# Paged attention behind three projections: the own keys' transpose in another place and another bank

## The chip, the cores and the metric

The kernel runs on one core of a Trainium2 chip, in one launch. The metric is the device time of that launch in microseconds. Before the change it is 2624.65 us, the median of three runs (2623.74 to 2630.95).

## The reference

`x` holds 64 sequences of 32 tokens of 512 numbers, in float32. Four layers are added to it, one after the other: a product with one of 8 weights for each sequence, two layers with low-rank adapters, and an attention layer. Only the last matters here:

```python
q = _rope(_rmsnorm(q, q_norm_w), pos)            # 32 query heads of 128
k = _rope(_rmsnorm(k, k_norm_w), pos)            # 8 key heads
kc = k_cache[block_table].reshape(bsz, L, HK, D) # 16 pages of 32 keys: L = 512
vc = v_cache[block_table].reshape(bsz, L, HK, D)
k_all = jnp.concatenate([kc, k], axis=1)         # 512 cached keys, then 32 own ones
v_all = jnp.concatenate([vc, v], axis=1)
scores = jnp.einsum('bqhd,bkhd->bhqk', q, k_all) * SCALE
scores = jnp.where(valid[:, None, None, :], scores, -1e+30)
probs = jax.nn.softmax(scores, axis=-1)
o = jnp.einsum('bhqk,bkhd->bqhd', probs, v_all)
return jnp.einsum('bse,de->bsd', o.reshape(bsz, seqlen, HQ * D), Wo)
```

## The kernel before, in words

The kernel has one program for each engine and sets all order by hand: each program is a list of instructions and of waits on semaphores, which other engines' instructions count up when they are done. I call such a count a mark.

The attention works in *units*: one sequence and one key head with its four query heads, so 128 rows of queries against 544 keys (512 cached, 32 own). There are 64 sequences x 8 heads = 512 units. The loop `pair` does two sequences, 16 units, in one turn (`in_pairs` writes the first and the last turn out and loops over the 30 between). I call one unit's share of each engine's program a *step*, and the 8 steps of one sequence a *half*, steps 0 to 7. In the code, `j` runs from 0 to 15, so step 7 is `j` = 7 or 15; behind `j` = 15 the loop turns. Units are taken in groups of four (`OG`): steps 0 to 3 and 4 to 7.

In step j TensorE (`tensor`, L1565 on) does:

- the scores of the unit two ahead (`scores`, L1348; three passes of a split product in each of two halves of the keys, L101 to L103). They go to bank pair j % 2 of `ps_s`; columns 384 to 511 of each bank are free of scores,
- the products of probabilities and values of the unit four behind (`outputs`, L1586; L1597 for cached keys, L1600 for own ones), into `ps_o`,
- the transposes of the probabilities of unit j against the cached keys (`transpose`, L1569; L1574), into `ps_pt`. In steps 3 and 7 the *own transpose* follows (L1580): the probabilities of the group's four units against their 32 own keys, which VectorE has gathered in `p_own`. It writes the spare columns of the odd bank pair (`spare`, L1254), and must not do so while VectorE reads that pair, hence the wait for `masked` (L1578). In step 7 the sums of the half's probabilities are transposed as well (`total`, L1582).

VectorE (`vector`) masks the scores of the unit two ahead and takes their maximum in one instruction (`mask_and_max`, L1319, named `att_prob<-both_ps_s,att_mask`), ahead of it gathers the own keys' probabilities of the unit one ahead (`gather`, L1508), splits keys and queries into a high and a low part (L1293), and copies finished outputs (L1530). At the start of steps 4 and 0 it copies the own transpose of the group before to `pto` (`copy_own`, L1515), and in step 0 it inverts the transposed sums into `inv` (`invert`, L1522). ScalarE takes the exponential (L1298), copies the transposed probabilities (L1476) and rounds the high parts (L1287).

GpSimd (`gpsimd`) issues, for each sequence in turn: the next queries and own keys (L1394, L1400), the next own values (L1412, four transfers), for which it waits until all products of the sequence before are done (`pv_done`, L1405), then four indirect gathers of the next values' pages (L1418), then the stores of the finished sequence (L1424, L1427). SyncE loads pages of keys. The last product of a sequence is done in step 3 of the next half.

The lines that matter for the waits are these:

```python
if j % OG == 3 and later(u, OG + 3):                     # scores, unit u = two ahead
    pe.wait_ge(pto_ready, UNITS // OG * i + j // OG)
if h == 3 and later(u, HK + 3):
    pe.wait_ge(inv_ready, 2 * i + p)
```

The first layer reads, on each engine, lists of places and adapters from memory into registers (`entries`, L191); on TensorE that is done once for four tiles.

## Time and profile before

| what | value |
| --- | --- |
| median of three runs | 2624.65 us (2623.74 to 2630.95) |
| span of the profiled execution | 2632.1 us |
| its mean granted TensorE clock | 0.979 of full speed |
| TensorE busy | 2449.5 us, 93% of the span |
| VectorE busy | 1799.6 us, 68% |
| ScalarE busy | 1587.4 us, 60% |
| GpSimd busy | 643.5 us, 24% |
| mean busy share of the 16 DMA engines, stretch 1400 to 1600 us | 0.82 |

The profile is of one execution, whose span, first to last instruction, is 2632.1 us; that is 7.5 us above the median of the timed runs and just above the slowest of them. A change of the sum that is made against the profiled execution is therefore carried over to the median as a difference. Times in the timelines are microseconds from the span's start. The attention fills the stretch from some 940 to 2235 us. The start of a TensorE row is taken from the hardware, its end is modelled, and matmuls overlap, so the length of a step is read from the start of one unit's scores to the start of the next one's.

### The profile page before, as it was taken

Reading aid. Unit: us, or ns where it says so; the run is one execution under the profiler, and the core shown is the slowest. Engines: PE = TensorE matmul, PEld = TensorE weight load, DVE = VectorE, ACT = ScalarE, POOL = GpSimd, SP = SyncE. Lnnn points to the kernel's source line nnn. Section 1 sums busy time; section 2 is a strip of 40 time slices with the busy share of each in tenths; the row PEclk is TensorE's granted clock in tenths of the full one; section 3 lists DMA queues with packets and bytes.
Section 4 is the critical chain, followed back from the end, with each engine's and each line's share of the span. In section 5 each row is a group of like instructions: output and inputs, shape, how many; then the busy total and the mean of one; then the engine's idle time right before and its main releaser. Section 6 shows DMA issues by size and latency. Waiting matters only on the chain. (4 is left out here: it accounts for less than half of the span.)

```text
span 2632.1 us, 55771 instructions
## 1 busy us (share of the span) xinstructions
PE 2449.5 (93%) x16326; PEld 2204.1 (84%) x16327; DVE 1799.6 (68%) x3690; ACT 1587.4 (60%) x3313; POOL 643.5 (24%) x932
## 2 busy tenths in 40 slices
PE   6799899999999889999999999999999999499999
PEld 5688688888888789999999998999999999388887
DVE  6445438999898967777777777777777776544443
ACT  3222237777787777777777777777777776311111
POOL 1222030000000134434443444344433442000000
PEclk9899899999999989999999999999999999799999
DMA  6422432333334388887888888887888883766664
GB/s 230 143 78 76 147 125 85 117 99 99 112 101 131 112 290 275 276 274 261 267 284 272 263 269 272 283 265 259 278 277 267 264 271 133 269 208 215 218 216 152
DMA packets 376143, 541.56 MB, mean 206 GB/s; under 512 B 49395, under 2 KB 263091, under 8 KB 372211
## 3 DMA queue, kind: packets, MB, share of 16 engines
q1 hardware_dynamic: 303922, 316.33, 37.9%
q0 software_dynamic: 70016, 221.30, 24.5%
q10 hardware_dynamic: 2112, 2.89, 0.4%
q8 instruction: 34, 0.56, 0.1%
q14 instruction: 59, 0.48, 0.1%
HBM read 442.06 MB, written 98.30 MB: 205 GB/s over the span
## 5 line engine op out<-in xcount | busy, mean ns | idle before, releaser
L1298 ACT ACTIVATE att_prob<-att_prob,att_shift 128x544 f32<-128x544 f32 x512 | 383.2, 748 | 262.2 <-DVE att_shift L1319 239.8
L1597 PE MATMUL both_ps_o<-att_pt,att_v 128*128 128x128 f32 x4096 | 540.0, 275 | 0.0
L1597 PEld LDWEIGHTS both_ps_o<-att_pt,att_v 128*128 128x128 f32 x4096 | 504.9, 191 | 0.0
L1319 DVE CUSTOM_DVE_ANT_0 att_prob<-both_ps_s,att_mask 128x544 f32<-128x544 f32 x512 | 365.5, 714 | 0.0
L101 PE MATMUL both_ps_s<-att_k_hi,att_q_hi 128*128 128x272 f32 x1024 | 340.5, 333 | 6.7 <-DVE att_k_lo L1293 5.2
L1293 DVE TENSOR_TENSOR att_k_lo<-att_k_raw,att_k_hi 128x1024 fp32r<-128x1024 f32 (+1 forms) x320 | 337.8, 1055 | 2.0 <-ACT att_k_hi L1287 1.9
L1476 ACT ACTIVATE att_pt<-both_ps_pt 128x512 f32<-128x512 f32 x512 | 296.8, 580 | 47.0 <-remote 43.6
L1574 PE MATMUL both_ps_pt<-both_ident,att_prob 128*128 128x128 f32 x2048 | 309.2, 274 | 7.6 <-ACT att_prob L1298 6.0
L1508 DVE COPY att_p_own<-att_prob 128x32 f32<-128x32 f32 x512 | 91.9, 180 | 324.6 <-PE both_ps_s L103 154.9
L1412 POOL DMA_DIRECT2D att_vo<-v_own x256 | 140.1, 547 | 651.8 <-PE both_ps_o L1600 589.1
L103 PE MATMUL both_ps_s<-att_k_hi,att_q_lo 128*128 128x272 f32 x1024 | 297.8, 291 | 0.0
L102 PE MATMUL both_ps_s<-att_k_lo,att_q_hi 128*128 128x272 f32 x1024 | 295.8, 289 | 0.0
L1287 ACT ACTIVATE att_k_hi<-att_k_raw 128x1024 fp32r<-128x1024 f32 (+1 forms) x320 | 292.9, 916 | 0.0
L1418 POOL DMA_INDIRECT att_v<-in_v_pages,att_rows_now x256 | 251.6, 983 | 85.9 <-issue 85.9
L1574 PEld LDWEIGHTS both_ps_pt<-both_ident,att_prob 128*128 128x128 f32 x2048 | 242.5, 142 | 8.3 <-ACT att_prob L1298 6.3
L101 PE MATMUL out_ps_y<-out_w_hi,out_o_hi 128*128 128x512 f32 x512 | 203.1, 397 | 37.3 <-DVE out_w_lo L1773 31.9
L1753 ACT ACTIVATE out_o_hi<-out_o 128x2048 fp32r<-128x2048 f32 x32 | 61.4, 1918 | 290.9 <-DVE out_o L1780 282.5
L101 PEld LDWEIGHTS both_ps_s<-att_k_hi,att_q_hi 128*128 128x128 f32 x1024 | 195.2, 191 | 16.9 <-issue 9.2
L102 PE MATMUL out_ps_y<-out_w_lo,out_o_hi 128*128 128x512 f32 x512 | 202.0, 395 | 0.0
L103 PE MATMUL out_ps_y<-out_w_hi,out_o_lo 128*128 128x512 f32 x512 | 201.8, 394 | 0.0
L1600 PE MATMUL both_ps_o<-att_pto,att_vo 128*128 128x128 f32 x1024 | 198.6, 276 | 2.4 <-DVE att_pto L1515 2.4
L102 PEld LDWEIGHTS both_ps_s<-att_k_lo,att_q_hi 128*128 128x128 f32 x1024 | 196.4, 192 | 0.0
(191 smaller groups left out, 5169.0 us busy)
## 6 DMA issues: line engine op xcount, KB each, us to landing
att_k_raw<-in_k_pages SPq DMA_DIRECT2D x1024, 128.0 KB, 3.9
q_t<-qkv_out_t SPq DMA_DIRECT2D x128, 256.0 KB
att_q_raw<-q_t POOLq DMA_DIRECT2D x64, 512.0 KB, 7.1
o_t<-att_o POOLq DMA_DIRECT2D x64, 512.0 KB, 6.9
out_o<-o_t SPq DMA_DIRECT2D x32, 1024.0 KB, 6.7
out_inv<-inv_t SPq DMA_DIRECT2D x32, 1024.0 KB, 6.7
qkv_w_stage<-in_w_qkv SPq DMA_DIRECT2D x12, 1024.0 KB, 5.2
l_w_stage<-in_w SPq DMA_DIRECT2D x8, 1024.0 KB, 6.8
```

Of the source, the lines that this page charges most:

```text
L101: pe.matmul(out, xh, wh, start=start, stop=False)
L102: pe.matmul(out, xh, wl, start=False, stop=False)
L103: return pe.matmul(out, xl, wh, start=False, stop=stop)
L1287: act.activation(hi, raw, ACT.Copy).then_inc(hi_done, 1)
L1293: dve.tensor_tensor(lo, raw, f32(hi), ALU.subtract).then_inc(lo_done, 1)
L1298: act.activation(prob[:, b, :], prob[:, b, :], ACT.Exp, bias=shift[:, b:b + 1], scale=-1.0, accum_out=total[:, j // HK, j % HK:j % HK + 1] ...
L1319: dve.tensor_tensor_reduce(out=prob[:, b, :].rearrange("p (a n) -> p a n", a=2), in0=ps_s[:, j % 2, :, 0:HALF], in1=mask[:, j // HK, :].re ...
L1418: pool.indirect_dma_start(v_sb[p][:, c, :], None, v_pages.rearrange("n k x -> (n k) x"), bass.IndirectOffsetOnAxis(ap=rows_now[:, p, c:c + ...
L1476: act.activation(pt_sb[:, j % OG, :, :], ps_pt[:, j % 2, :, :], ACT.Copy).then_inc(pt_ready, 1)
L1574: mm = pe.transpose(ps_pt[:, j % 2, c, :], prob[:, j % NB_P, c * P:(c + 1) * P], ident[:, :])
L1597: pe.matmul(out, v_sb[p][:, c, h * DH:(h + 1) * DH], pt_sb[:, j % OG, c, :], start=(c == 0), stop=False)
L1600: pe.matmul(out, vo_sb[p][:, g % 2, j % OG, :], pto_sb[:, g % 2, :], start=False, stop=True).then_inc(pv_done, 1)
```

## The change

Four things are done. First, the own transpose of a group and, in step 7, the one of the sums leave `transpose` and become `transpose_own`, which stands right behind the step's scores, ahead of the products and of the other transposes. Second, `spare` now names columns of the even bank pair, so the wait is for the masking of the unit one ahead (even) in place of the one two ahead (odd), and the scores that must wait for the copies are those of steps 4 and 0 (`j % OG == 2`, `h == 2`, where `j` is the unit two ahead) in place of steps 5 and 1. The transposes have a mark of their own, `own_t_done`. Third, the sums are inverted where they lie, 128 x 8 (`invert`, step 6, behind the masking), the inverse is transposed, and `copy_inv` copies it, 8 x 128, to `inv`. Fourth, VectorE's `copy_own` and `copy_inv` move from the start of steps 4 and 0 to steps 3 and 7, behind their masking. The last turn's two separate calls fall away.

Beside that TensorE's first lists of adapters in the first layer are read with a bounds check; three semaphores are merged into others or dropped in the layers before (renames, not shown).

```diff
@@ -188,11 +188,11 @@
         y_ready = m.sem("y_ready")
         y_stored = m.sems("y_stored", XB)
 
-        def entries(buf, first, n, engine, top):
+        def entries(buf, first, n, engine, top, waited=False):
 
             return nc.values_load_multi_w_load_instructions(
                 buf[0:1, bass.ds(first, n)], engines=[engine], min_val=0, max_val=top,
-                skip_runtime_bounds_check_because="the sort gives places within these")[1]
+                skip_runtime_bounds_check_because=None if waited else "the sort gives places within these")[1]
 
         def tiles(eng, body):
 
@@ -431,7 +431,8 @@
                 def tile(i, j):
                     if j == 0:
                         n = XB if is_tile(XB * (i + 1)) else NT0 % XB
-                        adapters[:] = entries(adapter, XB * i, n, mybir.EngineType.PE, NAD0 - 1)
+                        adapters[:] = entries(adapter, XB * i, n, mybir.EngineType.PE, NAD0 - 1,
+                                              waited=not later(XB * i, NAD0))
                     multiply(XB * i + j, j % 2, adapters[j])
                     if is_tile(XB * i + j + 2):
                         transpose(i + (j + 2) // XB, (j + 2) % XB)
...
@@ -1216,7 +1217,7 @@
     k_raw, q_raw, k_hi, q_hi, q_lo, k_lo = zip(keys_and_queries(first, 0), keys_and_queries(rest, 1))
     v0, vo0 = rest.sb("v0", [P, NPP // PPP, HK * DH]), rest.sb("vo0", [P, HK // OG, OG, DH])
     mask, prob = rest.sb("mask", [P, 2, NALL]), rest.sb("prob", [P, NB_P, NALL])
-    shift, total = rest.sb("shift", [P, NB_P]), rest.sb("total", [P, 2, HK])
+    shift, total, inv_q = rest.sb("shift", [P, NB_P]), rest.sb("total", [P, 2, HK]), rest.sb("inv_q", [P, 2, HK])
     rest.reach(AFTER_TAIL)
     o_sb, pt_sb = rest.sb("o", [P, 2, HK, P]), rest.sb("pt", [P, OG, NKEY // P, P])
     p_own, pto_sb, inv_sb = rest.sb("p_own", [P, 2, OG, SEQ]), rest.sb("pto", [P, 2, P]), rest.sb("inv", [HK, 2, P])
@@ -1232,8 +1233,8 @@
     hi_done, lo_done = m.sem("hi_done"), m.sem("lo_done")
     s_done = m.sem("s_done")
     masked = m.sem("masked")
-    exp_done, gathered = m.sem("exp_done"), m.sem("gathered")
-    t_done = m.sem("t_done")
+    exp_done, gathered, inverted = m.sem("exp_done"), m.sem("gathered"), m.sem("inverted")
+    t_done, own_t_done = m.sem("t_done"), m.sem("own_t_done")
     pt_ready, pto_ready = m.sem("pt_ready"), m.sem("pto_ready")
     pv_done = m.sem("pv_done")
     o_ready, inv_ready = m.sem("o_ready"), m.sem("inv_ready")
@@ -1253,7 +1254,7 @@
 
     def spare(half, rows):
 
-        return ps_s[0:rows, 1, half, D - P:D]
+        return ps_s[0:rows, 0, half, D - P:D]
 
     def load_pages(sp, s, p, c):
 
@@ -1351,9 +1352,9 @@
             pe.wait_ge(lo_done, PIECES * (2 * i + p + 1))
         if later(u, 2):
             pe.wait_ge(masked, u - 1)
-        if j % OG == 3 and later(u, OG + 3):
+        if j % OG == 2 and later(u, OG + 2):
             pe.wait_ge(pto_ready, UNITS // OG * i + j // OG)
-        if h == 3 and later(u, HK + 3):
+        if h == 2 and later(u, HK + 2):
             pe.wait_ge(inv_ready, 2 * i + p)
         for half in range(2):
             keys = slice(half * HALF, (half + 1) * HALF)
@@ -1509,17 +1510,22 @@
 
         def copy_own(i, g):
 
-            dve.wait_ge(t_done, UNITS * i + OG * (g + 1))
+            dve.wait_ge(own_t_done, UNITS // OG * i + g + 1)
             if later(i, 1) or g >= 2:
                 dve.wait_ge(pv_done, UNITS * i + OG * (g - 1))
             dve.tensor_copy(pto_sb[:, g % 2, :], spare(1, P)).then_inc(pto_ready, 1)
 
         def invert(i, p):
 
-            dve.wait_ge(t_done, UNITS * i + HK * (p + 1))
+            dve.wait_ge(exp_done, UNITS * i + HK * (p + 1))
+            dve.reciprocal(inv_q[:, p, :], total[:, p, :]).then_inc(inverted, 1)
+
+        def copy_inv(i, p):
+
+            dve.wait_ge(own_t_done, UNITS // OG * i + HK // OG * (p + 1))
             if later(i, 1):
                 dve.wait_ge(inv_stored[p], 16 * i)
-            dve.reciprocal(inv_sb[:, p, :], spare(0, HK)).then_inc(inv_ready, 1)
+            dve.tensor_copy(inv_sb[:, p, :], spare(0, HK)).then_inc(inv_ready, 1)
 
         def copy_o(i, g):
 
@@ -1537,16 +1543,18 @@
         def pair(i, last):
             for j in range(UNITS):
                 u, s, p = UNITS * i + j, 2 * i + j // HK, j // HK
-                if j % OG == 0 and later(u, OG):
-                    copy_own(*group_before(i, j, 1))
-                    if j % HK == 0:
-                        invert(*group_before(i, j, 1)[:1], (1 - p))
                 if not (last and j >= UNITS - 2):
                     wait_for_scores(2 * i + (j + 2) // HK, u + 2, (j + 2) % UNITS)
                 if not (last and j >= UNITS - 1):
                     gather(u + 1, (j + 1) % UNITS)
                 if not (last and j >= UNITS - 2):
                     mask_and_max(dve, u + 2, (j + 2) % UNITS)
+                if j % HK == HK - 2:
+                    invert(i, p)
+                if j % OG == 3:
+                    copy_own(i, j // OG)
+                if j % HK == HK - 1:
+                    copy_inv(i, p)
                 if not later(u, HK - 1):
                     for c in FIRST_LO[j]:
                         lo_part(dve, 1, 1, c)
@@ -1557,30 +1565,31 @@
                 if j % OG == 1 and later(u, 2 * OG):
                     copy_o(*group_before(i, j, 2))
             if last:
-                copy_own(i, UNITS // OG - 1)
-                invert(i, 1)
                 copy_o(i, UNITS // OG - 2)
                 copy_o(i, UNITS // OG - 1)
 
         in_pairs(dve, NSEQ // 2, pair)
 
     def tensor(pe):
-        def transpose(u, j, last):
-            p, g = j // HK, j // OG
+        def transpose(u, j):
             pe.wait_ge(exp_done, u + 1)
             if later(u, 2):
                 pe.wait_ge(pt_ready, u - 1)
             for c in range(NKEY // P):
                 mm = pe.transpose(ps_pt[:, j % 2, c, :], prob[:, j % NB_P, c * P:(c + 1) * P], ident[:, :])
-            if j % OG == OG - 1:
-
-                if not (last and j == UNITS - 1):
-                    pe.wait_ge(masked, u + 3)
-                pe.wait_ge(gathered, u + 1)
-                mm = pe.transpose(spare(1, P), p_own[:, g % 2, :, :].rearrange("p u k -> p (u k)"), ident[:, :])
+            mm.then_inc(t_done, 1)
+
+        def transpose_own(i, u, j, last):
+
+            p, g = j // HK, j // OG
+            if not (last and j == UNITS - 1):
+                pe.wait_ge(masked, u + 2)
+            pe.wait_ge(gathered, u + 1)
+            mm = pe.transpose(spare(1, P), p_own[:, g % 2, :, :].rearrange("p u k -> p (u k)"), ident[:, :])
             if j % HK == HK - 1:
-                mm = pe.transpose(spare(0, HK), total[:, p, :], ident[:, :])
-            mm.then_inc(t_done, 1)
+                pe.wait_ge(inverted, 2 * i + p + 1)
+                mm = pe.transpose(spare(0, HK), inv_q[:, p, :], ident[:, :])
+            mm.then_inc(own_t_done, 1)
 
         def outputs(i, u, j):
             p, h, g = j // HK, j % HK, j // OG
@@ -1607,11 +1616,13 @@
                 u = UNITS * i + j
                 if not (last and j >= UNITS - 2):
                     scores(pe, i + (j + 2) // UNITS, u + 2, (j + 2) % UNITS)
+                if j % OG == OG - 1:
+                    transpose_own(i, u, j, last)
                 if j >= OG:
                     outputs(i, u - OG, j - OG)
                 elif later(u, OG):
                     outputs(i - 1, u - OG, UNITS - OG + j)
-                transpose(u, j, last)
+                transpose(u, j)
             if last:
                 for j in range(UNITS - OG, UNITS):
                     outputs(i, UNITS * i + j, j)
```

How the instructions move shows in the compiled order. TensorE in the first turn, from the last score pass of step 7's unit on, before (`both_ps_s` takes the scores and the own transposes, `both_ps_o` the outputs, `both_ps_pt` the transposed probabilities):

```order
L103 MATMUL both_ps_s<-att_k_hi_3520,att_q_lo_3522 128x272
L1597 MATMUL both_ps_o<-att_pt,att_v_3524 128x128 [waits att_pt_ready]
L1597 MATMUL both_ps_o<-att_pt,att_v_3524 128x128 x3
L1600 MATMUL both_ps_o<-att_pto,att_vo_3525 128x128 [waits att_pto_ready]
L1574 MATMUL both_ps_pt<-both_ident,att_prob 128x128 [waits att_pt_ready,att_exp_done]
L1574 MATMUL both_ps_pt<-both_ident,att_prob 128x128 x3
L1580 MATMUL both_ps_s<-both_ident,att_p_own 128x128 [waits att_gathered,att_masked]
L1582 MATMUL both_ps_s<-both_ident,att_total 8x128
L101 MATMUL both_ps_s<-att_k_hi_3520,att_q_hi_3521 128x272 [waits att_masked]
```

and the same stretch now:

```order
L103 MATMUL both_ps_s<-att_k_hi_3576,att_q_lo_3578 128x272
L1588 MATMUL both_ps_s<-both_ident,att_p_own 128x128 [waits att_gathered,att_masked]
L1591 MATMUL both_ps_s<-both_ident,att_inv_q 8x128 [waits att_inverted]
L1606 MATMUL both_ps_o<-att_pt,att_v_3580 128x128 [waits att_pt_ready]
L1606 MATMUL both_ps_o<-att_pt,att_v_3580 128x128 x3
L1609 MATMUL both_ps_o<-att_pto,att_vo_3581 128x128 [waits att_pto_ready]
L1579 MATMUL both_ps_pt<-both_ident,att_prob 128x128 [waits att_pt_ready,att_exp_done]
L1579 MATMUL both_ps_pt<-both_ident,att_prob 128x128 x3
L101 MATMUL both_ps_s<-att_k_hi_3576,att_q_hi_3577 128x272 [waits att_inv_ready,att_pto_ready,att_masked]
```

The two transposes stand ahead of the products, and the scores behind step 7 wait for `att_pto_ready` and `att_inv_ready`.

VectorE inside the loop, from step 7 on, before (`ISA att_prob,att_shift` is the masking with the maximum, `att_p_own` the gathering of own keys, `att_k_lo` a low part of keys):

```order
L1501 REGISTER_ALU
L1508 COPY att_p_own<-att_prob 128x32 [waits att_exp_done,att_t_done,att_s_done]
L1319 ISA att_prob,att_shift<-both_ps_s,att_mask 128x544
L1319 ISA att_shift 128x1
L1292 ISA
L1293 TENSOR_TENSOR att_k_lo_3517<-att_k_raw_3512,att_k_hi_3514 128x4x8x32 [waits att_hi_done]
L1515 COPY att_pto<-both_ps_s 128x128 [waits att_pv_done,att_t_done]
L1522 RECIPROCAL att_inv<-both_ps_s 8x128 [waits pool_inv_stored0,att_t_done]
L1501 REGISTER_ALU
L1508 COPY att_p_own<-att_prob 128x32 [waits att_exp_done,att_t_done,att_s_done]
```

and now, from the end of step 6 on:

```order
L1521 RECIPROCAL att_inv_q<-att_total 128x8 [waits att_exp_done]
L1502 REGISTER_ALU
L1509 COPY att_p_own<-att_prob 128x32 [waits att_exp_done,att_t_done,att_s_done]
L1320 ISA att_prob,att_shift<-both_ps_s,att_mask 128x544
L1320 ISA att_shift 128x1
L1513 REGISTER_ALU
L1516 COPY att_pto<-both_ps_s 128x128 [waits att_pv_done,att_own_t_done]
L1528 COPY att_inv<-both_ps_s 8x128 [waits pool_inv_stored0,att_own_t_done]
L1293 ISA
L1294 TENSOR_TENSOR att_k_lo_3573<-att_k_raw_3568,att_k_hi_3570 128x4x8x32 [waits att_hi_done]
```

The inversion stands in step 6; the copies to `att_pto` and `att_inv` are behind step 7's masking and ahead of the low part, where before the copy and the inversion came behind that.

## Rows read from the trace of the kernel before

**Rows 1.** One stretch: its length, busy us (count) of each engine, clock, DMA share, GB/s.

```profile
1400.00:1600.00 200.00, 188.96 (x1614) 185.45 (x1614) 150.46 (x355) 152.85 (x297) 83.47 (x126) 1.00 0.82 269
```

**Rows 2.** The list of waits: who waited for whom, us in total, times, longest us.

```profile
POOL att_vo L1412 <- PE both_ps_o L1600: 589.1, 61, 15.9
...
PE both_ps_s L1580 <- DVE att_shift L1319: 70.5, 56, 1.4
...
PE both_ps_o L1600 <- DVE att_pto L1515: 2.4, 6, 0.5
```

**Rows 3.** Timeline of TensorE, end of a half: start us, us, instruction [idle before].

```profile
1435.51 0.37 PE L101 MATMUL both_ps_s<-att_k_hi,att_q_hi 128*128 128x272 f32 x1
...
1439.30 0.33 PE L1580 MATMUL both_ps_s<-both_ident,att_p_own 128*128 128x128 f32 x1 [1.24 <-DVE att_shift L1319]
...
1439.49 0.37 PE L101 MATMUL both_ps_s<-att_k_hi,att_q_hi 128*128 128x272 f32 x1
```

**Rows 4.** Timelines of VectorE and of ScalarE (last row), the same stretch.

```profile
1438.43 0.18 DVE L1508 COPY att_p_own<-att_prob 128x32 f32<-128x32 f32 x1 [3.00 <-remote]
1438.52 0.72 DVE L1319 CUSTOM_DVE_ANT_0 att_prob<-both_ps_s,att_mask 128x544 f32<-128x544 f32 x1
1439.16 0.08 DVE L1319 DVE_READ_ACCUMULATOR2_ANT att_shift<- 128x1 f32 x1
...
1440.30 0.28 DVE L1515 COPY att_pto<-both_ps_s 128x128 f32<-128x128 f32 x1
1440.50 0.94 DVE L1522 RECIPROCAL att_inv<-both_ps_s 8x128 f32<-8x128 f32 x1
...
1438.35 0.60 ACT L1476 ACTIVATE att_pt<-both_ps_pt 128x512 f32<-128x512 f32 x1 [1.09 <-remote]
```

**Rows 5.** Timeline of GpSimd: own values' load, gathers.

```profile
1415.76 0.94 POOL L1418 DMA_INDIRECT att_v<-in_v_pages,att_rows_now  x1 [0.31 <-issue]
...
1429.02 0.57 POOL L1412 DMA_DIRECT2D att_vo<-v_own  x1 [10.06 <-PE both_ps_o L1600]
...
1435.19 0.94 POOL L1418 DMA_INDIRECT att_v<-in_v_pages,att_rows_now  x1 [0.30 <-issue]
1436.43 0.94 POOL L1418 DMA_INDIRECT att_v<-in_v_pages,att_rows_now  x1 [0.30 <-issue]
```

**Rows 6.** Timelines of VectorE and TensorE, the half before, at the loop's turn.

```profile
1417.95 0.72 DVE L1319 CUSTOM_DVE_ANT_0 att_prob<-both_ps_s,att_mask 128x544 f32<-128x544 f32 x1
...
1419.24 0.39 PE L101 MATMUL both_ps_s<-att_k_hi,att_q_hi 128*128 128x272 f32 x1
```

**Rows 7.** Timelines of TensorE and VectorE (last row), steps 2 to 4 of a half.

```profile
1403.25 0.37 PE L101 MATMUL both_ps_s<-att_k_hi,att_q_hi 128*128 128x272 f32 x1
...
1405.56 0.37 PE L101 MATMUL both_ps_s<-att_k_hi,att_q_hi 128*128 128x272 f32 x1
...
1407.97 0.37 PE L101 MATMUL both_ps_s<-att_k_hi,att_q_hi 128*128 128x272 f32 x1
...
1406.69 0.72 DVE L1319 CUSTOM_DVE_ANT_0 att_prob<-both_ps_s,att_mask 128x544 f32<-128x544 f32 x1
```

**Rows 8.** Timelines of TensorE and VectorE (last row), a half whose hold is late.

```profile
1313.53 0.37 PE L101 MATMUL both_ps_s<-att_k_hi,att_q_hi 128*128 128x272 f32 x1
...
1316.06 0.37 PE L101 MATMUL both_ps_s<-att_k_hi,att_q_hi 128*128 128x272 f32 x1
...
1319.17 0.39 PE L101 MATMUL both_ps_s<-att_k_hi,att_q_hi 128*128 128x272 f32 x1
...
1317.98 0.29 DVE L1515 COPY att_pto<-both_ps_s 128x128 f32<-128x128 f32 x1 [1.45 <-remote]
```

**Rows 9.** Timeline of TensorE, steps 7 and 0, another half.

```profile
1130.48 0.38 PE L101 MATMUL both_ps_s<-att_k_hi,att_q_hi 128*128 128x272 f32 x1
...
1133.54 0.39 PE L101 MATMUL both_ps_s<-att_k_hi,att_q_hi 128*128 128x272 f32 x1
```

**Rows 10.** Line L193's small instructions: duration ns min/median/max.

```profile
L193 ACTq FUSED_REGOPS  x8: 51/51/57, 56.7 to 79.2; - x8
```

12 lines of the change are left out of this document (6 added, 6 removed).

## The prediction

> **What bounds the kernel now.** I read the stretches of the profile first: the change touches the attention, and there TensorE is busy 188.96 of 200 us, at a granted clock of 1.00 [rows 1]. Next comes the list of waits of TensorE, for it says what the other 11 us are. Nearly all of it is one line: L1580, the transpose of the own keys' probabilities, waits for L1319, VectorE's masking of a later unit: 70.5 us in 56 waits, up to 1.4 us each [rows 2]. There are 128 such transposes, so it is every second one.
>
> The timelines show which. In step 7 of a half TensorE starts the scores at 1435.51. The masking that reads them starts only at 1438.52, 3.01 us later, where in a calm step it takes 1.13 us (1405.56 to 1406.69) [rows 3, 4, 7], and the own transpose, which waits for the masking, starts at 1439.30 after 1.24 us idle; the next scores start at 1439.49 [rows 3]. A step without that lasts 2.31 us (1403.25 to 1405.56) [rows 7]; this one lasts 3.98.
>
> So the question is why the masking is 1.9 us late. VectorE has nothing else to do: it sat idle 3.00 us, and ScalarE 1.09 us at the same time, both released "remote" [rows 4]. GpSimd's timeline answers as far as the trace can: the four gathers of the values (L1418) go out in just these steps, the last starts at 1415.76 in one half and at 1436.43 in the next, and the masking of step 7 starts 2.19 and 2.09 us after it (1417.95, 1438.52) [rows 4, 5, 6]. I read it so: TensorE's marks to the other engines are held up while the gathers are issued and come free about 2 us behind the last one's start. And the gathers hang on TensorE in turn: GpSimd waited 61 times, 589 us, for L1600, the last product of the sequence before, in step 3 [rows 2]; from its first own-value load to the last gather's start it takes 7.41 us (1429.02 to 1436.43) [rows 5]. That is a ring: product in step 3, GpSimd, the late mark of step 7, masking, own transpose, the next scores, and three steps on the product again. Its round, not TensorE's work, is the length of a half.
>
> **The change, part by part.** (1) *Behind the masking of step 7.* Before, own transpose and totals' transpose follow the masking, then the scores. Now the transposes stand behind step 7's scores and wait for the masking of step 6, which is done; but the next scores wait for both copies, and VectorE has these behind the same late masking. So the wait is not removed, it is handed to the scores. New path from the masking's start: 0.64 us to its end (1438.52 to 1439.16), 0.20 from the start of the one PSUM reader to the start of the next (1440.30 to 1440.50), 0.28 for the second copy, 0.06 from a VectorE end to TensorE's start (1439.24 to 1439.30) [rows 3, 4]: 1.18 us. Old path inside the loop's body: 1438.52 to 1439.49, 0.97 us; at its turn, where TensorE's branch stands between transpose and scores, 1417.95 to 1419.24, 1.29 us [rows 4, 6]; the branch now runs during the wait. So +0.21 us in the one and -0.11 in the other. 56 of 63 halves have the stall [rows 2], half of them at the turn: 28 x 0.21 - 28 x 0.11 = +2.8 us.
>
> (2) *The own transpose in step 3* moves in front of the product that GpSimd waits for. A step with one own transpose is 0.10 us longer (1405.56 to 1407.97 against 2.31) [rows 7]. TensorE's work stays the same, but the ring's product comes 0.10 us later against it, so each held half grows by that: 56 x 0.10 = +5.6 us. If the ring is not rigid this is nothing; 0 is the lower bound.
>
> (3) *Halves with a late hold.* In one, the hold falls a step later. The own transposes stand right ahead of the scores of 1316.06, but VectorE could copy them only at 1317.98, after 1.45 us of waiting, TensorE waited for that copy in turn, and the step, 0 of the next half, lasted from 1316.06 to 1319.17, 3.11 us [rows 8]. Six such waits are in the list (L1600, 6 times) [rows 2]. With the transposes 2 us earlier their mark is out before the hold: 6 x (3.11 - 2.31) = -4.8 us.
>
> (4) *VectorE.* The inversion of 8 x 128 takes 0.94 us in step 0 [rows 4]; it goes, a copy of 8 x 128 comes, and an inversion of 128 x 8 in step 6. The trace has neither. The copy costs at least the 0.18 us of the 128x32 one and at most the 0.94 us of what it replaces; I take 0.28, since the 128x128 copy has the same 128 elements in a row [rows 4]. Over 56 halves the ends would be -6 and +37 us. The inversion, too, lies between 0.18 and 0.94 us, and with 8 elements in a row nearer to the first [rows 4]. Either fits in the 3 us that VectorE idles before step 7's masking, so nothing. The 0.94 us freed in step 0 shorten a masking that nobody waits for: nothing. In step 3 the copy now stands behind the masking, 1406.69 + 0.64 + 0.28 = 1407.61, ahead of the scores at 1407.97 [rows 7]: hidden by 0.3 us.
>
> (5) *The first layer* gets 16 small instructions on TensorE's queue, 0.051 us each as its like in the trace [rows 10]: 0.8 us if all show, 0 if the queue is ahead; I take 0.4. Renamed and merged semaphores cost nothing: no instruction is added.
>
> Sum: 2.8 + 5.6 - 4.8 + 0.4 = **+4.0 us** on the profiled execution's 2632.1 us, 2636.1 us; on the median of 2624.65 us, which lies 7.5 us below the profiled one, **2629 us**. A measurement of this kernel can tell about 0.3%, 7.9 us, from no change.
>
> A rule speaks against the change. The rows first: VectorE copies 128x32 from SBUF to SBUF in every step, GpSimd's gathers among them, and these start 1.24 us apart with 0.94 us each, while the only VectorE work near is such a copy [rows 4, 5]. The Trainium skill, "SBUF — State Buffer", in its warning on how VectorE blocks DMAs, says that such an operation in VectorE's two-port mode locks GpSimd out and that it can't write a DMA's descriptors meanwhile. That would make the new inversion a cost; the fourth rival has it.
>
> **Rivals.** *First, the hold misses step 7's mark.* Late is only the mark that is given inside the hold. In the half near 1130 the gathers lie differently and the scores of step 7 and 0 are 3.06 us apart (1130.48 to 1133.54) instead of 4; where the hold falls a step later they are 2.53 apart (1313.53 to 1316.06) [rows 8, 9]. The changed order shifts marks by 0.1 to 2 us. Against it: 0.1 us is little against what those halves differ by. A held step would last 1438.52 + 1.18 - 1435.51 = 4.19 us, so each half that gets free saves 1.66 us: a third of them (19) 32 us, 2597 us.
>
> *Second, the wait simply goes,* as the diff reads: -70.5 us, 2554 to 2558 us. Against it stands VectorE's order: both copies are behind the masking.
>
> *Third, slower: the own transposes' mark itself is late.* They now lie inside the hold with their own mark, behind that of the scores, and VectorE's copy waits for it. The masking hides 0.64 us of that; beyond it every 0.1 us costs 5.6 us. For it speaks how late their mark was at 1317.98 [rows 8]; against it, that after the hold VectorE and ScalarE, which wait for two different marks, started within 0.1 us of each other (1438.43, 1438.35) [rows 4]. One us behind the scores' mark: 0.36 x 56 = +20 us, 2649 us.
>
> *Fourth, slower: the inversion in step 6 stops GpSimd's gathers.* If it takes the 0.18 us of the 128x32 copy and delays the last gather by as much: 63 x 0.18 = +11 us more, 2640 us. Against it stand the even gathers. [...]
>
> **How the numbers follow.** Forecast 0.55, first rival 0.20, second 0.03, third 0.14, fourth 0.08. The forecast's own range is -3 to +11 us (the ring's 0.10 or nothing, the copy by 0.05 us either way), 2622 to 2636. Down to a third of the halves set free and up to most of the third rival gives 2598 to 2646. Slower by over 0.3%: a fourth of the forecast, third and fourth rival, 0.33 to 0.36, I say 0.33; faster: first and second rival and a little of the forecast, 0.25; within: 0.42.
>
> **What would show it.** Right, if L1580's wait for L1319 is gone and L101's scores wait instead, some 56 times and about as long, released by VectorE's copy; if step 7's masking still starts 2.1 us behind the last gather's start; if a held step lasts 4.2 us in body and turn alike; and if the six waits of L1600 are gone. Wrong, if the masking starts within 0.2 us of the scores' end in many halves, if the last two gathers start more than 1.35 us apart, or if VectorE's own copy waits for its mark after the masking's end.

## The result

| | median | range | runs |
| --- | --- | --- | --- |
| kernel before | 2625.64 us | 2623.74 to 2630.95 | 4 |
| changed kernel | 2637.47 us | 2635.94 to 2640.76 | 4 |

The ratio is 1.0043, with a 95% interval of 1.0028 to 1.0058. The change makes the kernel slower by 11.8 us, where the forecast was +4.0 us (2629 us). The range of 2598 to 2646 us holds it, and so does the direction of the forecast; its size was a third of the real one. Ratios here and below leave out two executions that were disturbed as a whole (6335 and 3542 us); the medians hold them.

### The profile page after: what moved, and what is told of

Read it like the earlier page. It is cut to its first block and busy times, and to the rows that moved or that the text cites. A ratio compares the mean times of both kernels' runs of the same rounds, so it can differ in the third digit from the quotient of the medians.

```text
span 2634.4 us, 55910 instructions
## 1 busy us (share of the span) xinstructions
PE 2443.3 (93%) x16326; PEld 2208.0 (84%) x16327; DVE 1780.4 (68%) x3754; ACT 1593.0 (60%) x3313; POOL 642.2 (24%) x932
## 5 line engine op out<-in xcount | busy, mean ns | idle before, releaser
L101 PE MATMUL both_ps_s<-att_k_hi,att_q_hi 128*128 128x272 f32 x1024 | 340.1, 332 | 87.1 <-DVE att_inv L1528 81.7
L1294 DVE TENSOR_TENSOR att_k_lo<-att_k_raw,att_k_hi 128x1024 fp32r<-128x1024 f32 (+1 forms) x320 | 338.4, 1057 | 2.1 <-ACT att_k_hi L1288 1.9
L101 PEld LDWEIGHTS both_ps_s<-att_k_hi,att_q_hi 128*128 128x128 f32 x1024 | 194.8, 190 | 101.7 <-DVE att_pto L1516 46.5
L101 PE MATMUL out_ps_y<-out_w_hi,out_o_hi 128*128 128x512 f32 x512 | 203.2, 397 | 36.9 <-DVE out_w_lo L1784 31.4
```

Of the source, the lines that this page charges most:

```text
L101: pe.matmul(out, xh, wh, start=start, stop=False)
L1294: dve.tensor_tensor(lo, raw, f32(hi), ALU.subtract).then_inc(lo_done, 1)
```

## The profile after

The stretch of 1400 to 1600 us of the changed kernel, as in [rows 1]: span, then busy us (count) of TensorE, its weight loads, VectorE, ScalarE and GpSimd, clock, DMA share, GB/s.

```profile
1400.00:1600.00 200.00, 186.63 (x1601) 184.37 (x1600) 149.57 (x368) 154.98 (x297) 82.53 (x127) 1.00 0.81 270
```

TensorE is busy 2.3 us less in it, at the same clock. The list of waits says where the idle time went; these rows answer to [rows 2]:

```profile
POOL att_vo L1413 <- PE both_ps_o L1609: 589.5, 61, 12.4
PE both_ps_s L101 <- DVE att_inv L1528: 81.7, 57, 1.6
```

The 56 waits of the own transpose for the masking are gone. 57 waits of the next unit's scores for VectorE's copy of the inverse stand in their place, 81.7 us in place of 70.5. The six waits of L1600 are gone too, as the third term had it.

TensorE at the end of a half inside the loop's body, then (behind the dots) at the loop's turn; step 7's scores, the two transposes, the next scores. This answers to [rows 3, 6].

```profile
1438.42 0.37 PE L101 MATMUL both_ps_s<-att_k_hi,att_q_hi 128*128 128x272 f32 x1
...
1439.27 0.27 PE L1588 MATMUL both_ps_s<-both_ident,att_p_own 128*128 128x128 f32 x1
1439.38 0.27 PE L1591 MATMUL both_ps_s<-both_ident,att_inv_q 128*8 128x128 f32 x1
...
1442.71 0.36 PE L101 MATMUL both_ps_s<-att_k_hi,att_q_hi 128*128 128x272 f32 x1 [1.29 <-DVE att_inv L1528]
```

```profile
1417.96 0.38 PE L101 MATMUL both_ps_s<-att_k_hi,att_q_hi 128*128 128x272 f32 x1
...
1422.14 0.39 PE L101 MATMUL both_ps_s<-att_k_hi,att_q_hi 128*128 128x272 f32 x1 [1.40 <-DVE att_inv L1528]
```

The held step lasts 1442.71 - 1438.42 = 4.29 us in the body and 1422.14 - 1417.96 = 4.18 us at the turn; forecast were 4.19 for both. The two transposes are issued long before. Over all held steps the medians are 4.31 us in the body and 4.23 us at the turn. VectorE in the same stretch, answering to [rows 4]:

```profile
1438.30 0.20 DVE L1521 RECIPROCAL att_inv_q<-att_total 128x8 f32<-128x8 f32 x1
1441.36 0.18 DVE L1509 COPY att_p_own<-att_prob 128x32 f32<-128x32 f32 x1 [2.85 <-remote]
1441.45 0.72 DVE L1320 CUSTOM_DVE_ANT_0 att_prob<-both_ps_s,att_mask 128x544 f32<-128x544 f32 x1
1442.09 0.08 DVE L1320 DVE_READ_ACCUMULATOR2_ANT att_shift<- 128x1 f32 x1
1442.09 0.28 DVE L1516 COPY att_pto<-both_ps_s 128x128 f32<-128x128 f32 x1
1442.29 0.27 DVE L1528 COPY att_inv<-both_ps_s 8x128 f32<-8x128 f32 x1
```

and GpSimd, answering to [rows 5]:

```profile
1432.05 0.56 POOL L1413 DMA_DIRECT2D att_vo<-v_own  x1 [9.93 <-PE both_ps_o L1609]
...
1438.14 0.94 POOL L1419 DMA_INDIRECT att_v<-in_v_pages,att_rows_now  x1 [0.30 <-issue]
1439.38 0.93 POOL L1419 DMA_INDIRECT att_v<-in_v_pages,att_rows_now  x1 [0.31 <-issue]
```

The masking still starts 1441.45 - 1438.42 = 3.03 us behind its scores' start and 2.07 us behind the last gather's (1439.38). The last gather starts 0.96 us behind step 7's scores, 0.92 before (1436.43 against 1435.51, [rows 3, 5]); the medians over the loop's held steps are 0.97 in body and turn now, and 0.92 and 0.87 before. The copies follow the masking in order, and the scores start 1.26 us behind the masking's start, at the turn 1422.14 - 1420.97 = 1.17 us:

```profile
1420.97 0.72 DVE L1320 CUSTOM_DVE_ANT_0 att_prob<-both_ps_s,att_mask 128x544 f32<-128x544 f32 x1
```

The trace also records when a semaphore is counted up, and that shows whose marks are late. Those of TensorE for the transposes and products of steps 6 and 7, whose modelled ends lie between 1438.67 and 1440.77, are counted one after the other from 1441.20 on, 0.05 to 0.07 us apart, the scores' at 1441.33 and the own transposes' at 1441.38. In between, VectorE's marks of 1438.39 and 1438.50 and ScalarE's of 1439.27 are counted 0.01 us after their instructions' ends. Taken over the whole trace, from the first gather's start of a burst to 2 us behind the last one's, 251 of TensorE's 360 recorded marks are counted more than 0.1 us late, and none of VectorE's 271 and ScalarE's 88. (Many marks given there have no record: 557, 400 and 262 were given.) So it is TensorE's marks that are held, and not the engines that wait for them.

The 128 x 8 inversion takes 0.20 us and the 8 x 128 copy 0.27. The inversion stands in the middle of a gather (1438.30), and the next gather still starts 1.24 us behind that one's start, the spacing of [rows 5]. Over the trace 36 third gathers of a burst have the inversion beside them and 26 have not; both kinds take 0.94 us.

A half with a late hold, answering to [rows 8]: steps 7, 0 and 1.

```profile
1317.03 0.37 PE L101 MATMUL both_ps_s<-att_k_hi,att_q_hi 128*128 128x272 f32 x1
1319.56 0.37 PE L101 MATMUL both_ps_s<-att_k_hi,att_q_hi 128*128 128x272 f32 x1
...
1321.87 0.37 PE L101 MATMUL both_ps_s<-att_k_hi,att_q_hi 128*128 128x272 f32 x1
```

Step 0 lasts 2.31 us where it lasted 3.11: the 0.8 us of the third term. But the half of [rows 9], which was cut short by luck (3.06 us for its step 7), now has a held step like the others, and so has the half at 1070, whose step 7 went from 2.76 to 3.70 us:

```profile
1132.19 0.38 PE L101 MATMUL both_ps_s<-att_k_hi,att_q_hi 128*128 128x272 f32 x1
...
1136.55 0.39 PE L101 MATMUL both_ps_s<-att_k_hi,att_q_hi 128*128 128x272 f32 x1 [1.59 <-DVE att_inv L1528]
```

So nearly every sign named ahead came true (the body's held step lasts 4.3 us and not 4.2), and yet the sum is off by 8 us. The experiments had two questions: which terms were mis-sized, and whether the held marks and the ring are what they were read to be.

## The experiments

Each kernel was run beside the kernel before on the same chip, and ratios are to that. This matters more than I knew, as the fifth and sixth run show.

### The first layer's bounds check alone, and the change without it

`l0_check_only` is the kernel before with this and nothing else:

```diff
-                        adapters[:] = entries(adapter, XB * i, n, mybir.EngineType.PE, NAD0 - 1)
+                        adapters[:] = entries(adapter, XB * i, n, mybir.EngineType.PE, NAD0 - 1,
+                                              waited=not later(XB * i, NAD0))
```

> The kernel before, with only the bounds check of the first layer's adapter lists taken from the change. Nothing is left out. Theory A (the check costs time on TensorE's path in the first layer, about 0.29 us for each of 8 entries, and what hangs on it): layer 0 ends 2 to 5 us later in the profile and the whole is 2 to 5 us longer than before, so about 2628 to 2631 us. Theory B (the check hides and the whole +11.8 us is the attention's): within 1 us of before. The attention's waits must be those of before, some 56 of the own transpose for the masking.

`no_check_const_wait` is the changed kernel with

```diff
-                        pe.wait_ge(w_split, a + 1)
+                        pe.wait_ge(w_split, t + 1)
...
-                                              waited=not later(XB * i, NAD0))
+                                              waited=False)
```

> The changed kernel, but TensorE's adapter lists are read without the bounds check, and the wait for the split weight of tile t counts to t + 1, a constant that is never less than the adapter's own number plus one. Theory A (the check costs 2 to 5 us): 2 to 5 us below the changed kernel, 2632 to 2635 us, unless the stricter wait costs some of it. Theory B: within 1 us of the changed kernel's 2637.5 us.

Measured: the first 2628.53 us, the ratio 1.0004 (0.9995 to 1.0013), so +1.1 us with an interval of -1.3 to +3.4; the second 2635.89 us, ratio 1.0038 (1.0025 to 1.0052), that is 0.0005 or 1.3 us below the changed kernel's 1.0043. Instructions of line L193 on TensorE's queue in the changed kernel, ns min/median/max:

```profile
L193 PEldq FUSED_REGOPS  x8: 146/148/165, 21.8 to 41.7; - x8
L193 PEldq SEQ_ASSERT  x8: 18/18/32, 22.0 to 41.9; - x8
```

Eight pairs of 0.148 + 0.018 us make 1.3 us, and 1.1 and 1.3 us are what the two runs give, though each interval reaches down to nothing. I had priced the 16 at 0.051 us each and taken half. That fits theory A in kind and neither proves it nor excludes theory B. The guess of 2 to 5 us was too high; it came from the end of the first layer in one profile of each kernel (98.2 us before, 102.8 us now), and that end is at 103.4 us in the run without the check too. By the second run's ratio most of the +11.8 us, some 10, is the attention's.

The first run gave something else: a second profile of an attention that is the same in every instruction as before. Body's and turn's held step, masking and last gather at the turn:

```profile
1398.56 0.37 PE L101 MATMUL both_ps_s<-att_k_hi,att_q_hi 128*128 128x272 f32 x1
1402.52 0.37 PE L101 MATMUL both_ps_s<-att_k_hi,att_q_hi 128*128 128x272 f32 x1
...
1418.77 0.38 PE L101 MATMUL both_ps_s<-att_k_hi,att_q_hi 128*128 128x272 f32 x1
...
1422.94 0.38 PE L101 MATMUL both_ps_s<-att_k_hi,att_q_hi 128*128 128x272 f32 x1
```

```profile
1421.70 0.72 DVE L1320 CUSTOM_DVE_ANT_0 att_prob<-both_ps_s,att_mask 128x544 f32<-128x544 f32 x1
```

```profile
1419.63 0.93 POOL L1419 DMA_INDIRECT att_v<-in_v_pages,att_rows_now  x1 [0.30 <-issue]
```

The held steps last 3.96 and 4.17 us, in the profile of before 4.06 and 4.35 (the medians over the loop's halves are 4.06 and 4.33, against 3.95 and 4.18 here). The masking comes 2.07 us behind the last gather's start at the turn, and came 2.19 us behind it in [rows 5, 6]; the medians are 2.07 here and 2.17 there. Two halves together take 40.66 us here (median of the 25 pairs from the seventh on, from the L101 rows), 40.91 in the profile I worked from, and 41.04 in the changed kernel. So the execution that I worked from had holds some 0.1 us longer, in over 50 halves. From its first scores to its last the attention lasts 1311.5 us in that execution, 1304.4 us in this one and 1309.9 us in the changed kernel. Two profiles of the same attention thus differ by 7.1 us, as much as the 7.5 us by which the first lay above the median. But the time ahead of the attention differs too, and the other way: 912.3 us in the first, 918.6 us in this one, 912 to 919 us in all profiles. Neither span alone says which is the usual one.

### The own transpose of step 3 behind the products

```diff
-                if j % OG == OG - 1:
+                if j % HK == HK - 1:
                     transpose_own(i, u, j, last)
...
+                if j % HK == OG - 1:
+                    transpose_own(i, u, j, last)
                 transpose(u, j)
```

> The changed kernel, but in step 3 (not in step 7) the own transpose stands behind the products again, still ahead of the unit's own transposes. Ring theory (term 2 of the sum: 0.10 us of TensorE's work ahead of the product that GpSimd waits for lengthens each held half): from step 7's scores to the last gather's start 0.10 us less, a pair of halves 0.2 us shorter, the whole 4 to 6 us faster than the changed kernel, about 2632 us. If the ring is not rigid: within 1.5 us of the changed kernel.

Measured: 2644.39 us, ratio 1.0074 (1.0060 to 1.0087), 8 us slower than the changed kernel and not 4 to 6 faster. The wait list shows that the edit did more than it should:

```profile
DVE att_pto L1516 <- PE both_ps_s L1588: 28.2, 63, 0.5
```

VectorE's copy now waits for the transpose in each half, and the scores behind the copy wait with it: step 3 lasts 2.61 us at the turn's halves (1414.99 to 1417.60 in its trace) and 2.69 us in the others, in place of 2.42 (1429.08 to 1431.50 in the changed kernel's).

```profile
1414.99 0.37 PE L101 MATMUL both_ps_s<-att_k_hi,att_q_hi 128*128 128x272 f32 x1
...
1417.60 0.39 PE L101 MATMUL both_ps_s<-att_k_hi,att_q_hi 128*128 128x272 f32 x1
```

The 0.19 to 0.27 us that this adds in step 3 outweigh the 0.10 us that the product gains, so the run says nothing for or against the ring. It does suggest why step 3's transpose was moved as well: with `spare` on the even bank the copy is due one step sooner, and behind the products the transpose costs 8 us.

### The copies ahead of the masking

```diff
+                if j % OG == 3:
+                    copy_own(i, j // OG)
+                if j % HK == HK - 1:
+                    copy_inv(i, p)
                 if not (last and j >= UNITS - 2):
                     mask_and_max(dve, u + 2, (j + 2) % UNITS)
                 if j % HK == HK - 2:
                     invert(i, p)
-                if j % OG == 3:
-                    copy_own(i, j // OG)
-                if j % HK == HK - 1:
-                    copy_inv(i, p)
```

> The changed kernel, but in steps 3 and 7 VectorE's copies of the own transpose and of the inverse stand ahead of the masking, in place of behind it. Theory of the handed-over wait (term 1: the scores of the next step wait for these copies behind the late masking, 0.64 + 0.20 + 0.28 us): if the own transposes' mark is out as early as the scores' mark, the held step falls from 4.2 to about 3.7 us, 56 x 0.5 = 28 us, 2610 us. The rival of the late mark (the own transposes' own mark is also held up, until about the same instant as the scores' mark): then the copies start when the hold ends, the masking 0.6 us behind, and the scores wait for the masking of the same bank's pair no more than for the copies: the same 3.7 us or a little more, but masking and exponential late by 0.5 us, 2610 to 2637 us. Slower than 2637 us only if the calm steps pay, where a copy now delays the masking by 0.3 to 0.5 us.

Measured: 2599.70 us, ratio 0.9902 (0.9887 to 0.9917): 37 us faster than the changed kernel and 27 us faster than the one before. TensorE's step 7 in the body, VectorE and the last gather:

```profile
1423.45 0.37 PE L101 MATMUL both_ps_s<-att_k_hi,att_q_hi 128*128 128x272 f32 x1
...
1427.22 0.36 PE L101 MATMUL both_ps_s<-att_k_hi,att_q_hi 128*128 128x272 f32 x1 [0.99 <-DVE att_inv L1528]
```

```profile
1426.60 0.29 DVE L1516 COPY att_pto<-both_ps_s 128x128 f32<-128x128 f32 x1
1426.80 0.27 DVE L1528 COPY att_inv<-both_ps_s 8x128 f32<-8x128 f32 x1
1427.00 0.70 DVE L1320 CUSTOM_DVE_ANT_0 att_prob<-both_ps_s,att_mask 128x544 f32<-128x544 f32 x1
```

```profile
1424.41 0.94 POOL L1419 DMA_INDIRECT att_v<-in_v_pages,att_rows_now  x1 [0.31 <-issue]
```

The held step is 3.77 us here. The copy starts 2.19 us behind the last gather's start, the masking of the changed kernel 2.07: the mark of the own transposes comes free at most 0.1 us behind that of the scores (they are counted at 1426.45 and 1426.40). The third rival is thereby refuted at its price of 1 us. The saving is 4.29 - 3.77 = 0.52 us in this step, and from pair to pair 41.04 - 39.91 = 1.13 us, 0.57 a half. Only held halves save; in the two traces 56 of them together give 32 us, and the whole attention is 31.7 us shorter (1278.2 us). The wait was handed over, as the first term says, and of the 0.64 us that the masking put between the hold's end and the scores nearly all could be taken out. The delay of the masking itself shows no cost in any other step.

### Work on the ring, and the same work beside it

Both kernels add four small transposes to step 3 of the changed kernel. `ring_work_ahead` repeats the own transpose, which stands ahead of the product that GpSimd waits for:

```diff
-            mm = pe.transpose(spare(1, P), p_own[:, g % 2, :, :].rearrange("p u k -> p (u k)"), ident[:, :])
+            for _ in range(5 if j % HK == OG - 1 else 1):
+                mm = pe.transpose(spare(1, P), p_own[:, g % 2, :, :].rearrange("p u k -> p (u k)"), ident[:, :])
```

> The changed kernel, but the own transpose of step 3 is done five times in place of once, ahead of the products: 4 x 0.10 = 0.4 us more of TensorE's work in each half, on the ring (ahead of the product that GpSimd waits for). Ring theory: the 64 halves grow by the whole 0.4 us, for the held ones wait for the hold and not for TensorE's work, and the others for TensorE: 64 x 0.4 = +26 us, about 2663 us; the held step stays at 4.2 us and more, and its wait does not shrink. If the ring is not rigid (the hold's place does not hang on that product) the wait of the held step shrinks by 0.4 us instead and the whole stays within 5 us of 2637 us.

`ring_work_behind` repeats a cached keys' transpose, behind the products:

```diff
-            for c in range(NKEY // P):
+            for c in [0] * (4 if j % HK == OG - 1 else 0) + list(range(NKEY // P)):
```

> The changed kernel with the same 0.4 us of extra work on TensorE in step 3, but behind the products: the first of the unit's four transposes of the probabilities is done four times more. Ring theory: this work lies between that product and step 7's scores, beside GpSimd's 7.4 us, so in 56 held halves the wait shrinks by 0.4 us and the length stays; only the 8 others grow, +3 us, about 2641 us. If TensorE's work as such sets the length: +26 us as in the run with the work ahead, 2663 us.

Measured: 2567.86 us and 2564.31 us, and the kernel before 2536.26 us (median of 19) beside them. This was another chip, and on it the kernel before is 90 us faster. The trace of `ring_work_ahead` there, step 7's scores and the next, the masking, the last gather:

```profile
1410.67 0.37 PE L101 MATMUL both_ps_s<-att_k_hi,att_q_hi 128*128 128x272 f32 x1
...
1413.20 0.37 PE L101 MATMUL both_ps_s<-att_k_hi,att_q_hi 128*128 128x272 f32 x1
```

```profile
1411.80 0.72 DVE L1320 CUSTOM_DVE_ANT_0 att_prob<-both_ps_s,att_mask 128x544 f32<-128x544 f32 x1
```

```profile
1411.64 0.94 POOL L1419 DMA_INDIRECT att_v<-in_v_pages,att_rows_now  x1 [0.30 <-issue]
```

The gathers go out at the same place, 0.97 us behind the scores, and take the same 0.94 us, but the masking starts 1.13 us behind the scores, as in a calm step: no mark is held (of 559 recorded marks of TensorE near the bursts, none is counted late), though the DMA engines are as busy (share 0.86 from 1400 to 1600 us). With no hold there is no ring, and the 0.4 us are paid wherever they stand (+31.6 and +28.1 us over the kernel before, 64 halves of 19.22 us in place of 18.78). Both were then run on chips that do hold marks.

> The same kernel as before (step 3's own transpose five times, 0.4 us more on TensorE ahead of the product that GpSimd waits for), since the last four runs fell on a chip on which no mark is held up at all and the kernel before takes 2536 us. If the kernel before takes some 2626 us here: ring theory +26 us over the changed kernel, 2663 us, with the held step's wait no shorter; if the ring is not rigid, within 5 us of 2637 us. If the kernel before takes some 2536 us here, this takes 2568 us again and tells nothing of the ring.

> Again the 0.4 us of extra work of TensorE in step 3 behind the products (a transpose of the unit's probabilities four times more), for a chip that holds marks up. Ahead of the product the same work took the ratio to the kernel before from 1.0043 to 1.0133, +24 us. Ring theory: behind it, it lies beside GpSimd's 7.4 us, the held step shrinks by 0.4 us and the length stays but for the 8 halves without a stall: +3 us over the changed kernel, ratio 1.005 to 1.007. If TensorE's work as such sets the length: ratio 1.013 again. If the kernel before takes 2536 us here, it tells nothing new.

Measured: ahead 2668.24 us, ratio 1.0133 (1.0118 to 1.0149), so 0.0090 or 24 us above the changed kernel; behind 2647.06 us, ratio 1.0075 (1.0058 to 1.0092), 0.0032 or 8 us above it. With the intervals of both ratios I estimate 18 to 29 us and 2 to 14 us; the two were run on different chips, and each is set against the kernel before on its own. The waits of the next scores, ahead:

```profile
PE both_ps_s L101 <- DVE att_inv L1528: 86.0, 57, 1.8
```

and behind, with one wait of VectorE:

```profile
PE both_ps_s L101 <- DVE att_inv L1528: 29.8, 56, 2.0
DVE att_p_own L1509 <- ACT att_prob L1299: 38.1, 35, 8.1
```

Ahead of the product the wait did not shrink (86.0 us against 81.7), the held step lasts 4.41 us (1412.47 to 1416.88), and the pair of halves grew from 41.04 to 42.10 us, 0.53 a half. Of that 0.44 us are the added work in step 3 (2.86 us in place of 2.42), and the rest is a later mark: the masking starts 2.16 us behind the last gather's start there and 2.08 in the changed kernel (medians). Behind the product the held step shrank to 3.84 at the turn and 4.08 us in the body (medians) and the pair grew by 0.25 us only. The place of the gathers shows the ring directly. The last gather starts 0.97 us behind step 7's scores in the changed kernel, 0.98 us with the work ahead of the product and 0.63 us with it behind (medians): ahead, the work moves the gathers with it, behind, it does not. The second term rests on this: what comes later at the product comes later at the hold.

The behind variant cost 8 us and not 3. Two things show. GpSimd's own way is 0.1 us longer (its second gather takes 1.06 us in place of 0.97). And step 6's scores now give their mark inside the hold, so that step 6's masking is some 2.1 us late, and behind it the exponential; VectorE's gathering ahead of step 7's masking waits for that 35 times, against 5 in the changed kernel. From the masking to the scores it takes 1.26 and 1.17 us as before. What the own transposes cost there is not shown.

### No gathers

The kernel before, with the first layer's check; the values of the first two sequences serve for all, so the later values are left out.

```diff
-            for c in range(NPP // PPP):
+            for c in range(NPP // PPP if not later(s, 2) else 0):
                 pool.indirect_dma_start(
...
-                    pe.wait_ge(v_loaded[p], 16 * (NPP // PPP) * (i + 1))
+                    pe.wait_ge(v_loaded[p], 16 * (NPP // PPP))
```

> The kernel before (with the first layer's bounds check of the change), but GpSimd gathers the pages of the values for the first two sequences only; all later ones are multiplied with these, so their values are left out. Theory (TensorE's marks are held up only while gathers are issued): no masking is late, no step lasts 4 us, a half lasts about 18.7 us, as the halves whose hold falls elsewhere do now, so 62 x 1.6 = -100 us, about 2527 us. Rival (the late marks are from something else, such as SyncE's loads or the stores): the waits of the own transpose for the masking stay, and less than 20 us is gained.

> The changed kernel with the same left out (the values' pages are gathered for the first two sequences only). Theory (the whole difference between the two kernels is in how the hold is met): without a hold the two orders of work cost the same, within 2 us of the kernel before without gathers. Rival (the change costs something in the calm steps too): it is 5 to 12 us slower than that one.

Both fell on the chip without holds: 2537.40 us, ratio 1.0006 (0.9997 to 1.0016), and 2539.35 us, ratio 1.0019 (1.0009 to 1.0028). They say two things even so. There the gathers cost nothing that can be seen, since the kernel with them takes 2536.26 us. And the two orders of work cost nearly the same when nothing is held: a half lasts 18.78 us in one trace and 18.79 in the other. The medians are 2 us apart, which by the spread of ten runs each may be anything from 0.3 to 3.5 us; the rival's 5 to 12 us are excluded. Then, on a chip with holds:

> Again the kernel before (with the first layer's bounds check) with gathers for the first two sequences only, whose values serve for all, for a chip that holds marks up. Theory (the gathers' issue holds up TensorE's marks): no masking later than 0.3 us in a half without gathers, 18.78 us per half, about 2536 us, the time that the kernel before has on a chip without held marks; ratio 0.96. Rival (the late marks come from the own values' loads or the stores): the 4 us steps stay, ratio above 0.99.

Measured: 2538.10 us, ratio 0.9657 (0.9640 to 0.9673), 90 us faster. The stretch, and steps 7 and 0 of a half:

```profile
1400.00:1600.00 200.00, 200.00 (x1739) 199.75 (x1738) 162.41 (x384) 165.59 (x319) 48.45 (x95) 1.00 0.59 184
```

```profile
1403.30 0.37 PE L101 MATMUL both_ps_s<-att_k_hi,att_q_hi 128*128 128x272 f32 x1
...
1405.83 0.37 PE L101 MATMUL both_ps_s<-att_k_hi,att_q_hi 128*128 128x272 f32 x1
```

TensorE is busy all of the 200 us, and step 7 lasts 2.53 us. On these chips the held marks are there when the gathers are there and gone without them, and they are worth 90 us, the same as the difference between the chips. One reserve: the run also takes load from the DMA engines (busy share 0.59 in place of 0.82), and doesn't tell GpSimd's issuing from the transfers themselves. The next run bears on the load.

### The gathers 1.2 us later

On top of the copies ahead of the masking, GpSimd's stores of the finished sequence go between the own values' load and the gathers:

```diff
                 if not (last and p):
                     load_own_v(s + 1, 1 - p)
-                    load_v(s + 1, 1 - p)
                 if later(s, 1):
                     store(s - 1, 1 - p)
+                if not (last and p):
+                    load_v(s + 1, 1 - p)
```

> The changed kernel with VectorE's two copies ahead of the masking (2600 us by itself), and GpSimd's stores of the finished sequence between the own values' load and the four gathers, in place of behind them: the gathers start 1.2 us later. On a chip with held marks: step 7's mark then falls between gathers, where the trace shows marks 0.1 to 1.25 us late and not 2, and the last gather holds step 0's mark, which has room; held steps of 2.5 to 3.7 us, so between 2540 and 2600 us. If the hold is on whatever mark comes in a burst of gathers until 2 us behind the last, the masking of step 7 is late by 3 us and the whole is 1.2 x 56 = 67 us longer, 2667 us. On a chip without held marks: within 3 us of the kernel before's 2536 us, for nothing waits.

Measured: 2557.64 us, ratio 0.9709 (0.9696 to 0.9722), 75 us faster than the kernel before on the same chip, which takes 2632.55 us there. The stretch, then steps 7, 0 and 1 on TensorE, the maskings of 7 and 0, the first and the last gather:

```profile
1400.00:1600.00 200.00, 197.33 (x1696) 195.11 (x1695) 159.33 (x392) 162.16 (x316) 98.37 (x133) 1.00 0.88 289
```

```profile
1432.42 0.38 PE L101 MATMUL both_ps_s<-att_k_hi,att_q_hi 128*128 128x272 f32 x1
1434.95 0.37 PE L101 MATMUL both_ps_s<-att_k_hi,att_q_hi 128*128 128x272 f32 x1
1437.26 0.38 PE L101 MATMUL both_ps_s<-att_k_hi,att_q_hi 128*128 128x272 f32 x1
```

```profile
1434.09 0.70 DVE L1320 CUSTOM_DVE_ANT_0 att_prob<-both_ps_s,att_mask 128x544 f32<-128x544 f32 x1
1439.04 0.72 DVE L1320 CUSTOM_DVE_ANT_0 att_prob<-both_ps_s,att_mask 128x544 f32<-128x544 f32 x1
```

```profile
1432.91 1.01 POOL L1419 DMA_INDIRECT att_v<-in_v_pages,att_rows_now  x1 [0.30 <-issue]
...
1437.06 0.94 POOL L1419 DMA_INDIRECT att_v<-in_v_pages,att_rows_now  x1 [0.30 <-issue]
```

No step 7 is held any more: all are 2.53 us long. The hold moved with the gathers. In the half shown it falls on step 0, whose masking starts 1439.04 - 1434.95 = 4.09 us behind its scores, again 1.98 us behind the last gather's start; the median over the halves is 2.12 us behind the scores. Step 0 itself can bear that, because no copy and no transpose hangs on its mark: the next scores start after 2.31 us. The gathers are all there and the DMA share is the highest of all (0.88), so it is where the gathers fall that counts and not how busy the DMA engines are on the whole. GpSimd's issuing and the transfers that it starts moved together, though, and are not told apart by this run either. To the kernel without gathers 14 us remain by the ratios. In the trace they are in some 20 halves where the late masking of step 0 reaches later steps; in the half shown step 3 lasts 3.21 us. The stores ahead of the gathers alone, without the copies ahead of the masking, were not run.

## Why the prediction was right in kind and short in size

By its own steps:

- *What bounds the kernel*: right. The hold comes with the gathers (90 us without them), and the ring stands (24 us against 8 for the same work on either side of the product).
- *Term 1, the wait is handed to the scores*, +2.8 us: right in place, and short in the body. From the masking's start to the scores it takes 1.26 us there, where I had 1.18, and 1.17 at the turn. The piece is the last one: I took 0.06 us from VectorE's end to TensorE's start, and from the end of the 0.27 us copy (1442.56) to 1442.71 it is 0.15. Over 28 halves 0.08 us is 2.2 us.
- *Term 2, 0.10 us on the ring*, +5.6 us: the mechanism holds, and the size is right at the turn only. The last gather comes later against step 7's scores by 0.10 us at the turn (0.87 to 0.97) and by 0.05 us in the body (0.92 to 0.97).
- *Terms 1 and 2 together* were to be 8.4 us. Summed over the 53 halves that are held in both traces, step 7 grew by 10.7 us against the second trace of the old attention, and by 4.2 us against the one that I had.
- *Term 3, the late holds*, -4.8 us: the six steps 0 did come back to 2.31 us, which saves 4.7 us against the second trace. What was missed is that two halves whose step 7 had been short by luck lost it: the half of [rows 9], 3.06 to 4.36 us, and the half at 1070, 2.76 to 3.70 us, which is one of the six. With the last half that is +2.8 us against the second trace. I had used the half of [rows 9] for the first rival only, as a sign of how marks slip free, and not as something to lose.
- *Term 4, VectorE*: right; copy 0.27 us (taken 0.28), inversion 0.20 us, hidden.
- *Term 5, the first layer*, +0.4 us: mis-sized. The bounds check takes 0.166 us an entry on TensorE's queue and not 2 x 0.051, 1.3 us in all. The timed runs give 1.1 and 1.3 us, with intervals that reach down to nothing.

Against the second trace that makes 10.7 - 4.7 + 2.8 us. The first two halves, which no term has, were 3.0 us shorter; they vary from kernel to kernel and run to run (27 to 31 us for the first alone), and I can't put that to the change. The attention as a whole is 5.5 us longer (1304.4 to 1309.9 us), and with the check the traces account for some 7 us. The measured 11.8 us has an interval of 7.4 to 15.2. The profile of the changed kernel is of the fastest of its four runs, 1.5 us under their median, and the second trace of one 2.8 us above its own (2631.30 against 2628.53 us), which can be the rest; it is not shown.

The step that fell short is therefore in how the sum was carried over. I wrote that the sum made against the profiled execution goes to the median as a difference. Against that execution it was not too small: its span is 2632.1 us, the changed kernel's 2634.4, where I had 2636.1, and the attention even got 1.6 us shorter. But that execution had holds 0.1 us longer than the second one (a turn of 4.33 against 4.18 us, a body of 4.06 against 3.95), and the changed kernel's profile has marks as early as the second one's: 2.08 us behind the last gather's start, against 2.17 and 2.07. In `ring_work_ahead` on another chip they come 2.16 us behind it. So such 0.1 us can differ from chip to chip or from execution to execution, and over 56 halves they outweigh the sum. That the forecast's size came within 8 us of the median owes something to luck: its terms were off in both directions.

The rivals: the first (halves set free) did not come; 57 waits are there, 56 before. The second (the wait simply goes) is refuted by the 81.7 us. The third (the own transposes' mark a microsecond late) is refuted by the copies ahead of the masking: 0.1 us. The fourth (the inversion stops the gathers) is refuted by their unchanged spacing of 1.24 us with the inversion in their midst. The rule of the Trainium skill on VectorE and GpSimd ("SBUF — State Buffer", the warning on how VectorE blocks DMAs) names a copy in float32 from SBUF to SBUF, and not an inversion; that it would hold for the inversion was my reading, and this trace does not bear it out: no gather is late by a 0.20 us inversion beside it. Nor did [rows 5] say much on it, since VectorE was idle beside the last gather. VectorE's work beside a gather can matter, though: in the five halves where the last gather runs beside a 1.2 us subtraction (L1294) it takes 1.56 us in place of 0.94.

## What to carry to other kernels

If the wait of an engine ends with an event that is late for a reason of its own, moving the waiting instruction may only hand the wait on; what can be won is the work between the late event and the next thing that needs it (37 us here, by copies put ahead of the masking), or the coincidence itself, by moving the cause to a step on which nothing hangs (another 50 us, by the ratios of two chips). A loop over several engines shows when the same small work is added on both sides of the suspected link. And a difference of 0.2 us in a step that occurs 56 times can't be read from one execution on either side; a second profile of the same code could have shown the spread of 0.1 us beforehand.

## What the runs showed of the hardware that I had not expected

- The held marks are not on every chip. In four sets of runs on chips that hold them the kernel before took 2625.6, 2626.4, 2632.6 and 2628.3 us, and in one set on another chip 2536.3 us (19 runs), where the trace of `ring_work_ahead` has the gathers' issue in the same place and of the same length. The kernel's time is a statement about the chip as well: 90 of 2626 us. That chip was used in one set only, so the chip and its state at that time are not told apart.
- On the chips that hold them, TensorE's marks that fall near the end of a burst of indirect gathers reach VectorE and ScalarE some 2.0 to 2.2 us behind the last one's start (1.98, 2.07, 2.07, 2.19 in the traces shown). VectorE's and ScalarE's own marks are on time there wherever they are recorded (271 and 88 in the changed kernel's trace). Why, and why not on every chip, stays open.
- A bounds check of a register that is loaded at run time costs TensorE's queue 0.148 + 0.018 us an entry.
